# One-hots of the edge sums read from a table, both bias rows written by VectorE, and W1's first half split by GpSimd, in a two-layer graph network kernel

## The chip, the cores and the metric

The kernel runs on one core of a Trainium2 chip. The metric is device time in microseconds (us) of that core, the median of several runs. A core has five engines with queues of their own: TensorE (PE; its weight loads are listed as PEld), VectorE (DVE), ScalarE (ACT), GpSimd (POOL) and SyncE (SP, which here only issues DMAs). They meet through semaphores. "PEq", "DVEq" and "SPq" are the sequencers of the queues.

## The reference, cut to what matters

```python
# x (1250, 512), src and dst (20000,), dst sorted, edge_attr (20000, 64), all float32
h  = relu(layernorm(x))
h0 = (1 + eps) * h + segment_sum(h[src], dst)
h0 = relu(batch_norm(h0 @ W01 + b01))        # 1024 wide
h0 = relu(batch_norm(h0 @ W02 + b02))        # 512 wide, the "second norm"
x  = x + h + h0
h  = relu(layernorm(x))
z1 = concat(h[src], h[dst], edge_attr) @ W1 + b1        # per edge
z2 = mish(z1) @ W2 + b2                                 # per edge
agg = segment_sum(mish(z2), dst)
u  = mish(concat(h, agg) @ W3 + b3)
x  = x + layernorm(h + u @ W4 + b4) * gamma + beta
```

## The kernel before, in words

Everything is float32. Products are made in three terms from operands split into a high part (rounded to the fast matmul type) and a low part (the rest), so each operand needs one cast and one subtraction ahead of its product. Every engine's program is written out by hand; its order is the order of the work, and nothing is scheduled by a planner.

**Stages**, in us of the profiled span: counting edges into a matrix of counts (0 to 92), the first product z0 (to 146), W01 with the first norm (`batch_norm` on VectorE, `move_product` on ScalarE; to 208), W02 with the second norm (to about 266), the layer norm and its transposes, then P = h @ W1[0:512] and Q = h @ W1[512:1024] for all nodes (`pq`, to 332), the first half of W3 with the first edge pairs between (to 365), the edge loop (to about 1020), the last products (to 1094).

**Norm stages.** A product runs feature block by feature block (`o`), each in four pieces (`b`) of 314 nodes. ScalarE moves a piece out of PSUM (line 1274), VectorE takes its statistics (1616). After the fourth piece VectorE aggregates (1621), ScalarE takes the root (1264), VectorE makes scale and shift in four tiny steps that each wait for the one before (1626 to 1629), and ScalarE applies them (1268). The high and low parts of the first norm's result are made on ScalarE (1361) and VectorE (2012) and feed the next product k block by k block. Meanwhile GpSimd splits the edge attributes (`attr_parts`, 724 and 729) in small blocks which SP stores to tables in HBM.

**W1.** ScalarE makes the high part of W1's eight k blocks (`w1_high`, 1378), the first four around the end of the second norm; GpSimd waits for the end of that norm and then makes the low parts (755). P's first product waits for the first four. Until then TensorE runs products that nobody reads (`idle_products`, 878), of which `IDLE_HT` = 4 and `IDLE_PQ` = 7 stand here.

**The edge loop.** A step works on pair `s`, 256 edges in two tiles of 128, 79 pairs in all. Steps are software-pipelined, and in the loops two steps (even and odd `s`) differ. In step `s`:
- TensorE: `z1(s)`, 8 transposes of gathered rows (1099) and 8 attribute products (1106); the second tile of `z2(s-2)` (12 products: 1124, 1125, 1129); the four products of the segment sum of pair `s-4` with its one-hot matrices (1156); the first tile of `z2(s-1)`.
- ScalarE: eight passes over 128x1024 for the two mish functions: 1431, 1435, 1439, then 1455 of pair `s-2`, then 1443, 1459, 1463, 1467.
- VectorE: `full1(s)` in two halves (`h_full`, 2107), high part of the message of `s-3` (2142), high part of h (2117), low part of the message (2146), `message(s-2)` (2132), the two one-hots of `s-2` (`hots1`, 1654), the row b2 into the PSUM bank of the first z2 tile of `s` (`b2_first_tile`, 2136), low part of h (2121). In even steps it then adds the segment sums of four tiles to the nodes (`add_group`, 1665, two instructions), which waits for the segment products of pair `s-3` (made in TensorE's odd step `s+1`), and loads the next group's row numbers into registers (1642).
- The b2 row of the second tile: ScalarE copies it in odd steps (`b2_second_tile`, 1470), for pairs of even number; for pairs of odd number TensorE adds it by a product with ones (1122).
- `z1(s)` waits for `h_full` of pair `s-1`, because both use the same PSUM banks; `full1(s)` waits for ScalarE's last pass on pair `s` (1443); ScalarE's first pass on `s` waits for `z1(s)`.
- GpSimd gathers rows of P and Q from HBM by indirect DMA (766, 774); SP loads the attribute parts (566), four pairs ahead.

## Time and profile before

| | us |
|---|---|
| median of 3 runs | 1096.25 (1095.99 to 1096.29) |
| the profiled execution, its own time | 1095.75 |
| its span, first to last instruction | 1093.9 |
| granted TensorE clock, mean | 0.989 of full speed |
| busy in the span: PE / DVE / ACT / POOL | 1037.2 / 864.4 / 886.2 / 717.4 |

1.85 us of the profiled execution lie around its span. Busy shares are averages over stages with different limits; matmuls overlap each other in the records (a 128x512 product is listed at 0.39 us and the next one starts 0.23 us later), so distances between starts are what counts on TensorE. On VectorE and ScalarE, too, a start can lie a little before the end of the instruction ahead.

### The profile page before, as it was taken

How to read it: one execution, taken by the hardware profiler on the slowest of the kernel's cores; microseconds unless marked ns; L12 is line 12 of the kernel's file. 1: busy time of each engine (PE TensorE's matmuls, PEld its weight loads, DVE VectorE, ACT ScalarE, POOL GpSimd, SP SyncE). 2: the span in 40 equal slices, each digit the busy share in tenths (PEclk: the TensorE clock that was granted, in tenths of full speed). 3: DMA queues.
4: the chain of work that ended last, by engine and by line, in shares of the span. 5: the costliest groups of instructions: out<-in, count | busy, mean ns of one | idle time of the engine just before them, and what ended most of it. 6: DMA issues, size and time to landing. Idle time of an engine off the chain costs nothing.

```text
span 1093.9 us, 18566 instructions
## 1 busy us (share of the span) xinstructions
PE 1037.2 (95%) x5633; PEld 873.0 (80%) x5634; DVE 864.4 (79%) x1500; ACT 886.2 (81%) x1081; POOL 717.4 (66%) x622
## 2 busy tenths in 40 slices
PE   3668999999999999999999999999999999999997
PEld 1226889998889878888888888888888888888796
DVE  7998536635526389999999999999999999999686
ACT  6985735624603699999999999999999999999584
POOL 6874448553255587777777777777777777760227
PEclk9969999999999999999999999999999999999999
DMA  2006962773165387776666676666666666661002
GB/s 106 9 1 151 173 217 93 247 228 116 71 227 119 86 187 161 161 166 136 139 143 146 136 142 145 139 139 138 148 139 138 143 147 134 140 135 39 1 1 95
DMA packets 82914, 141.63 MB, mean 129 GB/s; under 512 B 11115, under 2 KB 39020, under 8 KB 82742
## 3 DMA queue, kind: packets, MB, share of 16 engines
q0 software_dynamic: 38048, 87.58, 39.8%
q1 hardware_dynamic: 44822, 53.52, 15.3%
q8 instruction: 21, 0.34, 0.1%
q14 instruction: 23, 0.19, 0.1%
HBM read 115.42 MB, written 20.39 MB: 124 GB/s over the span
## 4 chain that ended last, share of the span: by engine, by line
PE 85%; DVE 7%; ACT 3%; issue 2%; POOL 1%; DVEq 1%; DMA 1%; ACTq 0%; POOLq 0%
PE banks L1124 12%; PE banks L1125 12%; PE banks L1129 12%; PE banks L1023 9%; PE banks L1156 7%; PE banks L1106 7%; PE banks L1099 6%; PE banks L1066 5%; PE banks L941 4%; PE banks L1087 4%; DVE edge_counts L1799 2%; PE banks L1219 2%; DVE key_onehot L1738 1%; PE banks L996 1%; PE banks L1122 1%
## 5 line engine op out<-in xcount | busy, mean ns | idle before, releaser
L774 POOL DMA_INDIRECT gather_pq<-q_table,dst x157 | 325.2, 2071 | 57.1 <-issue 47.5
L766 POOL DMA_INDIRECT gather_pq<-p_table,src x157 | 174.9, 1114 | 118.6 <-PE banks L1106 67.6
L1124 PE MATMUL banks<-w_lo,h_hi 128*128 128x512 f32 x620 | 242.0, 390 | 0.0
L1125 PE MATMUL banks<-w_hi,h_hi 128*128 128x512 f32 x620 | 241.7, 390 | 0.0
L1129 PE MATMUL banks<-w_hi,h_lo 128*128 128x512 f32 x620 | 166.1, 390 | 0.0
L1129 PEld LDWEIGHTS banks<-w_hi,h_lo 128*128 128x128 f32 x620 | 116.4, 188 | 24.4
L1125 PEld LDWEIGHTS banks<-w_hi,h_hi 128*128 128x128 f32 x620 | 116.4, 188 | 23.7
L1124 PEld LDWEIGHTS banks<-w_lo,h_hi 128*128 128x128 f32 x620 | 116.4, 188 | 23.5 <-issue 0.8
L2107 DVE SCALAR_TENSOR_TENSOR h_full<-mish_work,banks 128x512 f32<-128x512 f32 (+1 forms) x154 | 98.4, 680 | 45.0 <-ACT mish_work L1443 41.2
L2132 DVE SCALAR_TENSOR_TENSOR message<-mish_work,banks 128x1024 f32<-128x1024 f32 x78 | 95.3, 1221 | 8.4 <-ACT mish_work L1467 0.3
L1099 PE MATMUL banks<-ident,gather_pq 128*128 128x128 f32 x628 | 96.5, 275 | 1.5 <-DVE h_full L2107 0.9
L1106 PE MATMUL banks<-edge_attr_parts,we_hi 128*128 128x256 f32 (+1 forms) x316 | 94.6, 321 | 0.0
L2146 DVE TENSOR_TENSOR message_lo<-message,message_hi 128x1024 fp32r<-128x1024 f32 x77 | 93.1, 1209 | 0.0
L2121 DVE TENSOR_TENSOR h_lo<-h_full,h_hi 128x1024 fp32r<-128x1024 f32 (+1 forms) x77 | 93.0, 1208 | 0.0
L1099 PEld LDWEIGHTS banks<-ident,gather_pq 128*128 128x128 f32 x628 | 72.0, 140 | 18.2 <-DVE h_full L2107 11.7
L1467 ACT ACTIVATE mish_work<-mish_work 128x1024 f32<-128x1024 f32 (+1 forms) x79 | 83.5, 1057 | 2.5
L1463 ACT ACTIVATE mish_work<-mish_work 128x1024 f32<-128x1024 f32 (+1 forms) x79 | 83.2, 1054 | 1.3
L1431 ACT ACTIVATE mish_work<-banks 128x1024 f32<-128x1024 f32 (+1 forms) x77 | 78.6, 1021 | 6.7 <-PE banks L1106 5.8
L1435 ACT ACTIVATE mish_work<-mish_work 128x1024 f32<-128x1024 f32 (+1 forms) x77 | 81.4, 1057 | 2.5
L1439 ACT ACTIVATE mish_work<-mish_work 128x1024 f32<-128x1024 f32 (+1 forms) x77 | 81.3, 1056 | 2.4
L1459 ACT ACTIVATE mish_work<-mish_work 128x1024 f32<-128x1024 f32 (+1 forms) x79 | 82.5, 1044 | 0.1
L1106 PE MATMUL banks<-edge_attr_parts,we_lo 128*128 128x256 f32 (+1 forms) x316 | 81.6, 280 | 0.0
(268 smaller groups left out, 2610.6 us busy)
## 6 DMA issues: line engine op xcount, KB each, us to landing
edge_attr<-in_edge_attr_t SPq DMA_DIRECT2D x20, 256.0 KB, 2.9
attr_high<-edge_attr_hi SPq DMA_DIRECT2D x40, 128.0 KB, 2.1
attr_low<-edge_attr_lo SPq DMA_DIRECT2D x40, 128.0 KB, 1.8
edge_attr_parts<-attr_high SPq DMA_DIRECT2D x79, 64.0 KB, 2.8
edge_attr_parts<-attr_low SPq DMA_DIRECT2D x79, 64.0 KB, 3.7
x_nodes<-h_hi POOLq DMA_DIRECT2D x10, 256.0 KB, 15.0
x_nodes<-h_lo POOLq DMA_DIRECT2D x10, 256.0 KB, 7.8
p_table<-p_stage SPq DMA_DIRECT2D x10, 256.0 KB, 2.0
```

Of the source, the lines that this page charges most:

```text
L766: nc.gpsimd.indirect_dma_start(GP[:, 2 * j + k, :], None, p_tab[:, :], bass.IndirectOffsetOnAxis(ap=SRC[:, 2 * s + k:2 * s + k + 1], axis= ...
L774: nc.gpsimd.indirect_dma_start(GP[:, 2 * j + k, :], None, q_tab[:, :], bass.IndirectOffsetOnAxis(ap=DST[:, 2 * s + k:2 * s + k + 1], axis= ...
L1023: mm = pe.matmul(bank, weights[w][:, k, o * P:(o + 1) * P], acts[a](k)[:, nodes], start=(k == 0 and n == 0), stop=(k == kn - 1 and n == 2) ...
L1099: pe.matmul(Z1v[:, c, k * P:(k + 1) * P], GP[:, 2 * slot + k, c * P:(c + 1) * P], IDENT[:, :], is_transpose=True, skip_group_check=True, s ...
L1106: mm = pe.matmul(Z1v[:, c, 0:P * tiles(s)], w[:, c * P:(c + 1) * P], AT_R[:, slot, 0:P * tiles(s)], skip_group_check=True, start=False, st ...
L1124: pe.matmul(at, h_high(s, j)[:, c, e], W2_LO[:, c, :], start=False, stop=False, skip_group_check=True)
L1125: pe.matmul(at, h_high(s, j)[:, c, e], W2_HI[:, c, :], start=False, stop=False, skip_group_check=True)
L1129: mm = pe.matmul(at, h_low(s, j)[:, c, e], W2_HI[:, c, :], start=False, stop=(c == KD - 1), skip_group_check=True)
L2107: nc.vector.scalar_tensor_tensor(h_full_of(s)[:, at[0], at[1]], z1_work(s)[:, at[0], at[1]], -0.5, Z1v[:, at[0], at[1]], ALU.add, ALU.mult ...
L2121: nc.vector.tensor_tensor(h_low(s, j)[:, :, 0:P * tiles(s)], h_full_of(s)[:, :, 0:P * tiles(s)], h_high(s, j)[:, :, 0:P * tiles(s)].bitcas ...
L2132: nc.vector.scalar_tensor_tensor(MSG[:, :, :], EB[:, :, :], -0.5, z2_out(s, j), ALU.add, ALU.mult).then_inc(msg_full, 1)
L2146: nc.vector.tensor_tensor(MSG_LO[:, :, :], MSG[:, :, :], MSG_HI[:, :, :].bitcast(F32), ALU.subtract).then_inc(msg_lo, 1)
```

## The change

- **One-hots from a table.** The one-hots of the edge sums are no longer made in the edge loop. `four_hots` makes those of four tiles with one VectorE instruction (128x512), between the pieces of both norms (22 and 7 times) and behind each of the ten pieces of Q; ScalarE stores each of the 39 blocks (256 KB) to a new table in HBM (`store_hots`); the two staging slots lie in the upper part of the `iota` tile, which GpSimd writes again before the edge loop. In the edge loop SP loads 128 KB per pair, once the sums of two pairs before are made, behind the attribute loads of a pair six further on.
- **b2.** `b2_both_tiles` writes the row into both PSUM banks with one VectorE instruction (128x1024, right behind `message`); ScalarE's copies and the products with ones go, for all pairs from the third.
- **W1.** GpSimd makes high and low parts of the first four k blocks itself: two blocks when the attribute parts are done, the high parts of two more once those are stored, their low parts behind the end of the second norm. ScalarE keeps the high parts of the last four. `IDLE_HT` is 3 and `IDLE_PQ` 4; ScalarE moves the first transposed block ahead of the second root of the layer norm; the load of the b2 row moves behind the stores of P.
- **Scale and shift** in both norms: one of the waits between the four tiny steps goes.

```diff
-IDLE_HT, IDLE_PQ = 4, 7
+IDLE_HT, IDLE_PQ = 3, 4
+HOT_PIECES_1 = [(o, b) for o in range(KH) for b in range(3) if b != 1 or o in (0, 1, 4, 5, 6, 7)]
+HOT_PIECES_2 = [(o, b) for o in range(KD) for b in (0, 2) if (o, b) != (KD - 1, 2)]
 ...
+            def further_hots(q, j):
+                sp.wait_ge(seg_done, q - 1)
+                hots(q, j)
 ...
             for nt in range(NT):
                 sp.wait_ge(q_moved, nt + 1)
                 sp.dma_start(q_tab[nt * P:(nt + 1) * P, :], AGG[:, nt, :]).then_inc(q_stored, 16)
 ...
+            for j in range(2):
+                sp.wait_ge(hots_stored[j], 16 * ((HOT_GROUPS + 1 - j) // 2))
+            for q in range(2):
+                hots(q, q)
 ...
                 for j in range(SLOTS):
                     further_attributes(SLOTS * i + j, j)
+                    further_hots(SLOTS * i + j - HOTS_BEHIND, j % 2)
 ...
-                if after(s, 2) and k == 0:
-                    pe.wait_ge(b2_first, s - 1)
-                elif after(s, 2) and j == 0:
-                    pe.wait_ge(b2_second, s)
+                if after(s, 2):
+                    if k == 0:
+                        pe.wait_ge(b2_seeded, s - 1)
                 else:
                     pe.matmul(at, ONES_R[:, :], B2_R[:, :], start=True, stop=False, skip_group_check=True)
 ...
+                else:
+                    pe.wait_ge(hots_in[j], 16 * (group + 1))
 ...
+            def store_hots():
+
+                g = hots_sent[0]
+                hots_sent[0] += 1
+                act.wait_ge(hots_made, g + 1)
+                nc.scalar.dma_start(hot_tab[2 * g:2 * g + 2, :, :].rearrange("q p e -> p q e"),
+                                    HOTS4[:, g % 2, :, :].rearrange("p (q k) e -> p q (k e)", q=2)).then_inc(hots_stored[g % 2], 16)
 ...
+                        if (o, b - 1) in pieces:
+                            store_hots()
 ...
-                if j == 1 and after(s, 3) and live(s - 1) and tiles(s - 1) == 2:
-                    b2_second_tile(s - 1, 1 - j)
 ...
+            def four_hots():
+
+                g = hots_begun[0]
+                hots_begun[0] += 1
+                if g >= 2:
+                    dve.wait_ge(hots_stored[g % 2], 16 * (g // 2))
+                wide = [P, GROUP, P]
+                nc.vector.tensor_tensor(HOTS4[:, g % 2, :, :], IOTA[:, 0:P].rearrange("p (o k) -> p o k", o=1).broadcast_to(wide),
+                                        REL_G[:, GROUP * g:GROUP * (g + 1)].rearrange("p (t o) -> p t o", o=1).broadcast_to(wide),
+                                        ALU.is_equal).then_inc(hots_made, 1)
 ...
-            def b2_first_tile(s, j):
+            def b2_both_tiles(s, j):
                 dve.wait_ge(msg_full, s - 1)
-                nc.vector.tensor_copy(Z2[:, 2 * j, :], B2_ROW[:, 0, :]).then_inc(b2_first, 1)
+                nc.vector.tensor_copy(Z2[:, 2 * j:2 * j + 2, :], B2_ROW[:, :, :].broadcast_to([P, 2, DIM])).then_inc(b2_seeded, 1)
 ...
-                if live(s - 2):
-                    hots1(s - 2, j)
-                    if live(s):
-                        b2_first_tile(s, j)
+                if live(s - 2) and live(s):
+                    b2_both_tiles(s, j)
```

VectorE in the edge loop, an even step, from `message` to the segment sums; before:

```order
L2132 SCALAR_TENSOR_TENSOR message<-mish_work,banks 128x1024 [waits msg_lo,b_r]
L1654 ISA
L1654 TENSOR_SCALAR onehot<-iota,dst_in_group 128x128
L1654 ISA
L1654 TENSOR_SCALAR onehot<-iota,dst_in_group 128x128
L2136 COPY banks<-b_row 128x512 [waits msg_full]
L2121 TENSOR_TENSOR h_lo<-h_full,h_hi 128x1024 [waits h_hi]
L2152 REGISTER_ALU [waits xagg_done]
L1662 ISA [waits seg_done,agg_done]
L1665 REGISTER_ALU
L1665 SCALAR_TENSOR_TENSOR agg_nodes<-banks,from_low,agg_nodes 128x512
```

The same place after the change:

```order
L2234 TENSOR_TENSOR message_lo<-message,message_hi 128x1024 [waits msg_hi]
L2220 SCALAR_TENSOR_TENSOR message<-mish_work,banks 128x1024 [waits msg_lo,b_r]
L2224 COPY banks<-b_row 128x1024 [waits msg_full]
L2213 TENSOR_TENSOR h_lo<-h_full,h_hi 128x1024 [waits h_hi]
L2240 REGISTER_ALU [waits xagg_done]
L1752 ISA [waits seg_done,agg_done]
L1755 REGISTER_ALU
L1755 SCALAR_TENSOR_TENSOR agg_nodes<-banks,from_low,agg_nodes 128x512
```

Both one-hots are gone, the copy is twice as wide, and it now stands directly behind the instruction whose end (`msg_full`) it waits for.

GpSimd from the last attribute parts over the end of the second norm (`bn_ready`) to the gathers of P; before:

```order
L729 TENSOR_TENSOR edge_attr_lo<-edge_attr,edge_attr_hi 128x256 [waits attr_low_stored1,attr_hi]
L755 TENSOR_TENSOR w_lo<-weights_a,w_hi 128x512 [waits w1_hi_made,bn_ready]
L755 TENSOR_TENSOR w_lo<-weights_a,w_hi 128x512 [waits w1_hi_made] x7
L766 DMA gather_pq<-p_table,src 128x512 [waits p_stored,idx_in]
```

The same place after the change:

```order
L795 CAST w_hi_first_half<-weights_a 128x512 [waits w1_in,attr_lo]
L795 CAST w_hi_first_half<-weights_a 128x512
L799 TENSOR_TENSOR w_lo<-weights_a,w_hi_first_half 128x512 [waits w1_first_hi_made] x2
L795 CAST w_hi_first_half<-weights_a 128x512 [waits attr_low_stored0,attr_low_stored1,attr_high_stored1,attr_high_stored0]
L795 CAST w_hi_first_half<-weights_a 128x512
L799 TENSOR_TENSOR w_lo<-weights_a,w_hi_first_half 128x512 [waits w1_first_hi_made,bn_ready]
L799 TENSOR_TENSOR w_lo<-weights_a,w_hi_first_half 128x512 [waits w1_first_hi_made]
L817 TENSOR_TENSOR w_lo<-weights_a,w_hi 128x512 [waits w1_hi_made] x4
```

Six instructions now stand ahead of the end of the norm, and two instead of four of the low parts that P waits for stand behind it.

## Rows read from the trace of the kernel before

**Rows 1.** Busy time by engine: us, busy (count) per engine, clock, DMA, GB/s.

```profile
400.00:1010.00 610.00, 609.41 (x3239) 515.05 (x3238) 559.46 (x803) 600.15 (x621) 452.41 (x279) 1.00 0.67 140
```

**Rows 2.** TensorE in order of time, edge loop: start, us, instruction, count.

```profile
703.15 0.66 PE L1099 MATMUL banks<-ident,gather_pq 128*128 128x128 f32 x4
704.91 0.28 PE L1106 MATMUL banks<-edge_attr_parts,we_lo 128*128 128x256 f32 x1
...
711.45 0.60 PE L1099 MATMUL banks<-ident,gather_pq 128*128 128x128 f32 x4
...
713.26 0.40 PE L1122 MATMUL banks<-b_parts,ones 128*128 128x512 f32 x1
713.50 0.39 PE L1124 MATMUL banks<-w_lo,h_hi 128*128 128x512 f32 x1
...
716.92 0.39 PE L1156 MATMUL banks<-message_lo,onehot 128*128 128x512 f32 x1
```

**Rows 3.** ScalarE in the same stretch.

```profile
702.64 0.59 ACT L1470 COPY banks<-b_row 128x512 f32<-128x512 f32 x1
705.22 1.03 ACT L1431 ACTIVATE mish_work<-banks 128x1024 f32<-128x1024 f32 x1
```

**Rows 4.** VectorE in the same stretch.

```profile
702.41 1.28 DVE L2107 SCALAR_TENSOR_TENSOR h_full<-mish_work,banks 128x512 f32<-128x512 f32 x2
...
710.33 1.28 DVE L2107 SCALAR_TENSOR_TENSOR h_full<-mish_work,banks 128x512 f32<-128x512 f32 x2 [0.85 <-ACT mish_work L1443]
...
712.75 1.20 DVE L2146 TENSOR_TENSOR message_lo<-message,message_hi 128x1024 fp32r<-128x1024 f32 x1
714.05 1.22 DVE L2132 SCALAR_TENSOR_TENSOR message<-mish_work,banks 128x1024 f32<-128x1024 f32 x1
715.19 0.47 DVE L1654 TENSOR_SCALAR onehot<-iota,dst_in_group 128x128 fp32r<-128x128 f32 x2
715.59 0.68 DVE L2136 COPY banks<-b_row 128x512 f32<-128x512 f32 x1
716.18 1.21 DVE L2121 TENSOR_TENSOR h_lo<-h_full,h_hi 128x1024 fp32r<-128x1024 f32 x1
717.66 0.75 DVE L1665 SCALAR_TENSOR_TENSOR agg_nodes<-banks,from_low,agg_nodes 128x512 f32 x1 [0.26 <-issue]
```

**Rows 5.** Single lines over 400 to 1000: durations in ns (min/median/max), first and last start.

```profile
L1665 DVE SCALAR_TENSOR_TENSOR agg_nodes<-banks,from_low,agg_nodes x35: 750/751/752, 416.3 to 985.5; 128x512 f32 x35
```

**Rows 6.** VectorE, the first such sum, an earlier stretch of the edge loop.

```profile
397.56 1.22 DVE L2121 TENSOR_TENSOR h_lo<-h_full,h_hi 128x1024 fp32r<-128x1024 f32 x1
...
398.73 0.75 DVE L1665 SCALAR_TENSOR_TENSOR agg_nodes<-banks,from_low,agg_nodes 128x512 f32 x1
```

**Rows 7.** DVE's sequencer over 400 to 1000, the register load behind the sums.

```profile
L1642 DVEq TENSOR_LOAD <-tile_range x36: 743/748/1451, 399.3 to 986.1; - x36
```

**Rows 8.** All engines around the end of the second norm.

```profile
251.96 1.44 POOL L729 TENSOR_TENSOR edge_attr_lo<-edge_attr,edge_attr_hi 128x256 fp32r<-128x256 f32 x2
...
266.31 4.98 POOL L755 TENSOR_TENSOR w_lo<-weights_a,w_hi 128x512 fp32r<-128x512 f32 x4 [12.92 <-DVE bn_shift L1629]
...
269.24 0.83 DVE L1607 SCALAR_TENSOR_TENSOR ln_bias<-ln_mean_var,rstd 128x2 f32<-128x2 f32 x1
```

**Rows 9.** The same, a little later.

```profile
272.58 0.16 DVE L1607 SCALAR_TENSOR_TENSOR ln_bias<-ln_mean_var,rstd 128x4 f32<-128x4 f32 x1
272.76 0.69 DVE L1635 SCALAR_TENSOR_TENSOR h_t_lo<-banks,h_t_hi 128x512 fp32r<-128x512 f32 x1
...
273.80 0.39 PE L1066 MATMUL banks<-w_hi,h_t_lo 128*128 128x512 f32 x1
```

**Rows 10.** ScalarE and VectorE at the end of the first norm.

```profile
199.12 1.43 ACT L1268 ACTIVATE hidden_t<-hidden_t,bn_shift,bn_scale 128x1256 f32<-128x1256 f32 x1
200.99 0.49 DVE L1616 BATCH_NORM_STATS2 bn_stats<-hidden_t 128x6 f32<-128x314 f32 x1 [1.25 <-ACT hidden_t L1274]
...
202.70 0.48 DVE L1616 BATCH_NORM_STATS2 bn_stats<-hidden_t 128x6 f32<-128x308 f32 x1 [1.23 <-ACT hidden_t L1274]
```

**Rows 11.** DMA issues of the page: KB each, median us to landing.

```profile
edge_attr<-in_edge_attr_t SPq DMA_DIRECT2D x20, 256.0 KB, 2.9
```

**Rows 12.** TensorE at the first edge pair.

```profile
343.15 0.66 PE L1099 MATMUL banks<-ident,gather_pq 128*128 128x128 f32 x4 [0.53 <-DMA gather_pq<-q_table,dst]
```

More of the change, by code:

```diff
@@ L394, in gnn_kernel @@
         gat1 = [sem(f"gathered1_{j}") for j in range(SLOTS)]
-        hot_ready, seg_done, agg_done = sem("hot_ready"), sem("seg_done"), sem("agg_done")
+        seg_done, agg_done = sem("seg_done"), sem("agg_done")
+        hots_made, hots_stored, hots_in = sem("hots_made"), [sem(f"hots_stored{j}") for j in range(2)], [sem(f"hots_in{j}") for j in range(2)]
         last_hots = sem("last_hots")
@@ L751, in _, with w1_first_hi, w1_first_lo @@
             attr_parts(ATTR_FIRST, ALL_STEPS)
+            def w1_first_hi(k):
+                nc.gpsimd.tensor_copy(W1P_HI[:, k, :], WA[:, k, :]).then_inc(w1p_hi, 1)
+            def w1_first_lo(k):
+                pool.wait_ge(w1p_hi, k + 1)
+                nc.gpsimd.tensor_tensor(W1_LO[:, k, :], WA[:, k, :], W1P_HI[:, k, :].bitcast(F32), ALU.subtract).then_inc(w1_lo, 1)
+            pool.wait_ge(attr_lo, 2 * ALL_STEPS)
+            pool.wait_ge(w1_in, 16)
+            w1_first_hi(0)
+            w1_first_hi(1)
+            w1_first_lo(0)
+            w1_first_lo(1)
+            for stored in attr_stored:
+                for j in range(2):
+                    pool.wait_ge(stored[j], 16 * ALL_STEPS)
+            w1_first_hi(2)
+            w1_first_hi(3)
             pool.wait_ge(bn_ready, KH + KD)
-            for k in range(2 * KD):
-                pool.wait_ge(w1_hi, k + 1)
+            w1_first_lo(2)
+            w1_first_lo(3)
+            for k in range(KD, 2 * KD):
+                pool.wait_ge(w1_hi, k - KD + 1)
                 nc.gpsimd.tensor_tensor(W1_LO[:, k, :], WA[:, k, :], W1_HI[:, k, :].bitcast(F32), ALU.subtract).then_inc(w1_lo, 1)
@@ L790, in _ @@
                 gather_q(s)
+            for j in range(2):
+                pool.wait_ge(hots_stored[j], 16 * ((HOT_GROUPS + 1 - j) // 2))
+            nc.gpsimd.iota(IOTA[:, P:NP], [[1, NP - P]], base=P, channel_multiplier=0,
+                           allow_small_or_imprecise_dtypes=True).then_inc(pool_const, 1)
             for s in range(SLOTS, EDGE_PAIRS):
@@ L1064, in pq @@
                 for k in range(KD):
-                    for a, w in ((HT_LO, W1_HI), (HT_HI, W1_LO), (HT_HI, W1_HI)):
-                        mm = pe.matmul(Z2[:, 2 * part + nt % 2, :], a[:, k, nt * P:(nt + 1) * P], w[:, KD * part + k, :],
-                                       start=(k == 0 and a is HT_LO), stop=(k == KD - 1 and a is HT_HI and w is W1_HI))
+                    high = W1_HI[:, KD + k, :] if part else W1P_HI[:, k, :]
+                    for n, (a, w) in enumerate(((HT_LO, high), (HT_HI, W1_LO[:, KD * part + k, :]), (HT_HI, high))):
+                        mm = pe.matmul(Z2[:, 2 * part + nt % 2, :], a[:, k, nt * P:(nt + 1) * P], w,
+                                       start=(k == 0 and n == 0), stop=(k == KD - 1 and n == 2))
                 mm.then_inc(mm_done, 1)
@@ L1135, in _, with segment1 @@
             FINAL_ROWS = [FINAL_MSG.rearrange("p c e -> p (c e)")]
-            def segment1(s, j, last):
+            def segment1(s, j, last, group):
                 final = isinstance(s, int) and s == FINAL
@@ L1175, in edge_step @@
                 if live(s - 4):
-                    segment1(s - 4, j, j == 1 or isinstance(s, int) and s - 4 == EDGE_PAIRS - 1)
+                    segment1(s - 4, j, j == 1 or isinstance(s, int) and s - 4 == EDGE_PAIRS - 1, group)
                 if live(s - 1):
@@ L1425, in _ @@
             nc.scalar.preload_act_table_set("natural_log_exp_and_others")
+            for _ in range(HOT_TABLE):
+                store_hots()
+            assert hots_sent[0] == HOT_GROUPS
             def exp1(s):
@@ L2122, in lo1 @@
                                         h_high(s, j)[:, :, 0:P * tiles(s)].bitcast(F32), ALU.subtract).then_inc(h_lo, 1)
-            def hots1(s, j):
-                make_hots([ONEHOT[:, j, k, :] for k in range(2)], REL_G, 2 * s).then_inc(hot_ready, 1)
             def message(s, j):
```

79 lines of the change are left out of this document (52 added, 27 removed).

## The prediction

> **What bounds the kernel now.** Read first the busy time of the edge loop [rows 1]. In 610 us TensorE is busy for 609.4, ScalarE for 600.2, VectorE for 559.5: three engines that are nearly full, so the loop is bound by a round trip through several of them, and busy shares don't say which. The loop is also most of the kernel: the sums of line 1665 stand once in two pairs, and 34 of their intervals fill 985.5 - 416.3 us [rows 5], so two pairs take 16.74 us, and about 37 such periods follow each other.
>
> Read then who waits, in order of time, through one period. VectorE waits visibly only in even steps: h_full at 710.33 for ScalarE, 0.85 us [rows 4]. The other h_full, at 702.41, starts late behind the sums, and TensorE's transposes of the next pair start at 703.15 [rows 2], 0.74 later: half an h_full. That is TensorE's only stall in the period, and small: the record shows those four transposes 0.66 long and the unstalled ones at 711.45 0.60 long, and with the last 0.02 us of waiting it is about 0.08 in all. So TensorE alone needs 16.66 of 16.74.
>
> Two round trips can be read off, both through that h_full.
> - **Path B, by TensorE.** Transposes 703.15, last segment product 716.92 + 0.39 = 717.31 [rows 2], sums 717.66 (0.35 later), the next h_full 702.41 + 16.74 = 719.15 (1.49 later), transposes 0.74 later: 14.16 + 0.35 + 1.49 + 0.74 = 16.74. This path is tight.
> - **Path A, by VectorE and ScalarE.** h_full 710.33 to h_lo 716.18 is 5.85; from h_lo the sums could start 1.17 later, as they did at 398.73 behind the h_lo of 397.56 [rows 6], where they even overlap its end by 0.05; then 1.49 and 0.74 as above; transposes 703.15 to ScalarE's first pass 705.22 [rows 3] is 2.07; that to h_full 710.33 is 5.11. The sum is 16.43, so this path has 0.31 us to spare. The profile calls the 0.26 ahead of the sums "issue", which looks like VectorE's own time; I read it as the wait for TensorE.
>
> **The change part by part, edge loop.** *TensorE* loses the b2 product of every second pair: 713.50 - 713.26 = 0.24 per period [rows 2]. It lies in path B: 16.50. TensorE alone: 16.66 - 0.24 = 16.42. *ScalarE* loses its copy of 0.59 (702.64, rows 3). It is in no tight path: ScalarE's pass of 705.22 starts when the transposes and attribute products are done (704.91 + 0.28 = 705.19, rows 2), with or without the copy. Worth nothing. *VectorE*, per step: the two one-hots go, 715.59 - 715.19 = -0.40. The copy gets twice as wide: h_full moves 512 columns per instruction in 0.64 and message 1024 in 1.22, so I take 1.22 instead of 0.68: +0.54. And the copy now stands right behind the message whose end it waits for. Without such a wait the next start lies 1.14 behind the message's (715.19 - 714.05); message itself waits for the end of message_lo ahead of it and starts 1.30 behind that one's start (714.05 - 712.75, for 1.20 us of work) [rows 4]. So +0.18. Sum per step -0.40 + 0.54 + 0.18 = +0.32. In odd steps 0.85 us of waiting hides it. In even steps it lies in path A: 16.43 + 0.32 = 16.75.
>
> One link of path A gets shorter with it. The 1.49 from sums to h_full is not VectorE's work (two sums of 0.75 that overlap by 0.08 make 1.33 or so) but its sequencer's: behind the sums it loads registers for 0.75 us [rows 7], and that starts when TensorE's segment products are done. These come 0.24 earlier, the sums 0 to 0.1 later, so the load falls under the sums; the link is then between 1.32 and 1.49. Path A is between 16.58 and 16.75. I take 16.58, since in rows 6 the queue ran ahead of the engine. Against 16.74 that is 0.16 x 37 = **-5.9 us**; the ends are 0 and, if path B or TensorE alone is the bound, -0.24 x 37 = -8.9 to -0.32 x 37 = -11.8.
>
> The Trainium skill, "VectorE: DVE Perf Modes", section "The DRAIN you can't avoid", says that a semaphore between two VectorE instructions costs nothing extra and that only their number counts. By that the +0.18 would be zero, path A 16.40 and path B the bound, -8.9 us. Rows 4 speak against it: 1.30 with a wait, 1.14 without.
>
> The loads of the one-hots (128 KB per pair on SP, behind a wait for the sums of two pairs before) I cost at nothing: a load is issued after the segment products of one step and needed two steps later, two times 8.37 us, against 2.9 for 256 KB to land [rows 11]. The DMA engines are at 0.67 in the loop [rows 1]; 128 KB in 8.4 us is 16 GB/s on 140. If the cover were gone, TensorE would stall at the segment products, by what is missing, 37 times.
>
> **Norms.** *End of the second norm.* Of the low parts of W1, four run from 266.31 for 4.98 us [rows 8], and the tiny ln_bias at 269.24 takes 0.83 beside them, against 0.16 at 272.58 when GpSimd is idle [rows 9]. Two low parts remain there, done by about 268.9, so -0.67. The shorter chain and ScalarE's casts that go give 0.2 more. P starts at 273.80 behind h_t_lo (272.76 + 0.69) and seven idle products; with four of them h_t_lo decides, which gives 0.1. Together **-0.9**. Cover: GpSimd has 266.3 - 253.4 = 12.9 us free there [rows 8] and the six instructions put there need at most 6 x 1.25 = 7.5, at the price of the low parts. Ends: -1.4, and +2 if the attribute parts finish 7 us later because the stores of the one-hots (29 x 256 KB in 110 us) compete with theirs.
>
> *End of the first norm.* The last three blocks of one-hots stand between the last statistics. The store of the first one is issued behind ScalarE's apply, at 199.12 + 1.43 = 200.55 [rows 10], and lands 2.9 later [rows 11], 203.5. The third block uses the same slot, so VectorE, free at 201.5, waits until 203.5 and takes 0.69 more (as h_t_lo, also 128x512, rows 9), to 204.2; the last statistics (202.70) stand behind it, 1.4 late, and ScalarE, which has to issue the third store before its next high part (202.57), is late by as much. TensorE can start the second product with the blocks that are ready; how long they last no row here says, so I take half of the 1.4, **+0.7**, ends -0.3 (shorter chain, store lands in 2) and +2. In the middle of both norms the same waits occur, but TensorE writes into four banks and gets far ahead: nothing.
>
> *Q and the first pair.* TensorE waits 0.53 for the gather of the first pair [rows 12]; the last one-hot store and the first loads now run beside the last store of Q and that gather. All of it is on the path: **+0.5**, ends 0 and +2. The ten one-hot blocks of that stage stand behind what TensorE waits for: nothing.
>
> **The rivals.**
> 1. *TensorE's side is the bound* (the wait costs nothing, or the links overlap more): -8.9 - 0.9 + 0.7 + 0.5 = -8.6, to -11.5 with TensorE alone: 1087.6 to 1084.7. The page's rule on semaphores, above, leads to the first of the two.
> 2. *The sequencer sets the pace*: the link stays 1.49, path A is 16.75, the loop gains nothing: 0 + 0.3 = about 1096.6. For it: the two paths are then equal to the hundredth. Against it: rows 6.
> 3. *Slower: the idle ahead of the sums is VectorE's own.* Then path A has been tight at 16.74 all along, and the +0.32 adds to it: +11.8 + 0.3, or 1108.4. It decides from the point where h_lo's end, and not the last segment product, releases the sums. For it: the word "issue" in rows 4. Against it: rows 6, where no idle time is left.
> 4. *The stores hold up the norms*: attribute parts late, low parts of W1 late, first norm's end +2, first pair +2: the gain is eaten, 1095 to 1099.
>
> **How the numbers follow.** The profiled execution took 1095.75, the median 1096.25; the sum -5.9 - 0.9 + 0.7 + 0.5 = -5.6 is taken from the median: **1090.6**. Chances: forecast (1087.7 to 1094.0) 0.50, rival 1 0.15, rival 2 0.17, rival 3 0.08, rival 4 0.10. The range for 8 in 10 runs from TensorE's bound to rival 4, 1084.5 to 1098.5. A measurement tells about 0.2% (2.2 us) from no change. Faster: forecast and rival 1, 0.65. Within 0.2%: rival 2 and half of rival 4, 0.22. Slower: rival 3 and the other half, 0.13.
>
> **What the profile after would show.** Period of the sums 16.58 (16.50 or less: rival 1; 16.74: rival 2; 17.06: rival 3). Copy of 1024 columns 1.22 long, starting 1.3 behind message. Sums starting at h_lo's end less 0.05, with no idle time. TensorE stalled once per period by 0.15 to 0.2. No ScalarE copy of b2. P's first product about 0.9 earlier behind the second norm; the first norm's end up to 1 later. Wrong would make it above all a VectorE copy of another length, or segment products that wait for a table load.

## The result and the profile after

The changed kernel takes 1143.62 us (1140.15 to 1145.55), the kernel before, in the same session, 1096.27 (1095.99 to 1096.48): a ratio of 1.042, 95% interval 1.040 to 1.044. The forecast was 1090.6, the range 1084.5 to 1098.5, with 0.13 for slower. The measured time lies 53 us above the forecast, and on the other side of the kernel before.

The profiled execution took 1145.55, its span is 1143.7, 49.8 more than before. First the distance between matching instructions of both traces, to see in which stage the time went:

| stage | before | after | more |
|---|---|---|---|
| up to the first product of the first norm | 146.4 | 149.3 | 2.9 |
| that norm's products | 55.4 | 63.6 | 8.2 |
| to the first product with W1 | 72.0 | 76.4 | 4.4 |
| the products P and Q | 58.0 | 66.8 | 8.7 |
| from there to the first sum of the edge loop | 66.9 | 66.6 | -0.3 |
| first to last sum of the loop | 626.6 | 652.5 | 25.9 |

The first row is no effect of the change: the program up to there is the same, and in the kernels below that point lies anywhere from 146.7 to 149.7 (the latter in scan_before, which has nothing of the change). What is left has two parts: 26 us in the edge loop, 21 us ahead of it.

**The edge loop.** VectorE in the even step, from `message` (2220) to the next h_full (2199), in the trace of after; it answers to [rows 4].

```profile
750.90 1.22 DVE L2220 SCALAR_TENSOR_TENSOR message<-mish_work,banks 128x1024 f32<-128x1024 f32 x1
752.15 1.23 DVE L2224 COPY banks<-b_row 128x1024 f32<-128x1024 f32 x1
753.29 1.24 DVE L2213 TENSOR_TENSOR h_lo<-h_full,h_hi 128x1024 fp32r<-128x1024 f32 x1
754.45 0.74 DVE L1755 SCALAR_TENSOR_TENSOR agg_nodes<-banks,from_low,agg_nodes 128x512 f32 x1
755.11 0.74 DVE L1755 SCALAR_TENSOR_TENSOR agg_nodes<-banks,below_low,agg_nodes 128x512 f32 x1
756.88 1.29 DVE L2199 SCALAR_TENSOR_TENSOR h_full<-mish_work,banks 128x512 f32<-128x512 f32 x2 [1.03 <-issue]
```

Down to the sums this is the prediction: the copy is 1.23 long and starts 1.25 behind `message`, the sums start 0.08 before h_lo's end. But h_full stands 2.43 behind them, and not 1.32 (over the steady loop 1.76 to 2.53, median 2.36). What lies between is the register load on DVE's sequencer, with its durations in ns (min/median/max) from 400 to 1000; the row answers to [rows 7].

```profile
L1732 DVEq TENSOR_LOAD <-tile_range x34: 762/1600/1759, 403.4 to 983.4; - x34
```

It took 748 ns before and takes 1600 now, in the same place and for the same three words. TensorE stands still meanwhile; the waits of 400 to 1000 (us in total, times, longest) and its first transposes behind the h_full above:

```profile
PEld banks L1166 <- DVE h_full L2199: 37.7, 33, 1.4
ACT mish_work L1511 <- PE banks L1173: 34.7, 53, 1.2
DVE h_full L2199 <- issue: 29.1, 32, 1.1
...
757.62 0.66 PE L1166 MATMUL banks<-ident,gather_pq 128*128 128x128 f32 x4 [0.83 <-DVE h_full L2199]
```

Path A with what is measured: 16.43 + 0.27 for VectorE's step (from the end of message_lo to h_lo it is 2.50, in before 2.23) + (2.36 - 1.49) for the link = 17.57; the loads of the steady loop stand 17.53 apart. One row of before had already shown the price. Behind the very sum of [rows 6] the next h_full is this one of before, 2.21 later, and its load is the 1451 of [rows 7]:

```profile
400.94 1.28 DVE L2107 SCALAR_TENSOR_TENSOR h_full<-mish_work,banks 128x512 f32<-128x512 f32 x2 [0.80 <-issue]
```

**The first norm.** SP, VectorE, ScalarE and TensorE from 155 to 167, after:

```profile
155.64 1.94 SPq L556 DMA_DIRECT2D weights_b<-in_w  x4
...
165.03 0.69 DVE L1692 TENSOR_TENSOR onehots_of_group<-iota,dst_in_group 128x512 f32<-128x512 f32 x1 [6.50 <-DMA onehot_table<-onehots_of_group]
...
166.18 0.52 ACT L1352 ACTIVATE hidden_t<-banks,cols 128x314 f32<-128x314 f32 x1 [7.31 <-DVE onehots_of_group L1692]
...
166.97 0.60 PE L1089 MATMUL banks<-z_t_lo,w_hi 128*128 x1 [3.51 <-ACT hidden_t L1352]
```

The third block waits 6.5 us for the store of the first, issued at 156.93 between the third and the fourth load of 512 KB of weights (155.64 to 157.10). ScalarE waits for the block before it moves the next piece, and TensorE, four banks ahead, still stands for 3.5 us. Behind that its granted clock is 0.50 (1.2 of 2.4 GHz) from 167 to 170, against 1.00 in before, and the products are 0.26 apart instead of 0.145. Five short stands between 178 and 209, 2.4 us in all, make up the rest of the 8.2.

**P and Q.** VectorE and GpSimd ahead of the fifth piece of Q, and from the waits of 290 to 358 that of TensorE, after:

```profile
335.79 6.41 DVE L1692 TENSOR_TENSOR onehots_of_group<-iota,dst_in_group 128x512 f32<-128x512 f32 x1 [1.72 <-DMA onehot_table<-onehots_of_group]
342.12 0.68 DVE L2185 TENSOR_TENSOR agg_nodes<-banks,rows 128x512 f32<-128x512 f32 x1
...
334.48 2.29 POOL L846 CAST w_lo<-weights_a 128x512 fp32r<-128x512 f32 x4
336.73 4.92 POOL L849 TENSOR_TENSOR w_hi<-weights_a,w_lo 128x512 fp32r<-128x512 f32 x4
...
PE banks L1133 <- DVE agg_nodes L2185: 5.7, 1, 5.7
```

One block takes 6.41 us in place of 0.69. It starts while GpSimd works through eight instructions without a pause and ends 0.55 behind the last of them. Behind TensorE's wait of 5.7 us its granted clock is 0.50 from 343.0 to 347.7, and eleven products stand 0.43 apart instead of 0.23: that is 2.2 us more of the 8.7.

### The profile page after: what moved, and what is told of

The parts are those of the page before. It is cut to its first block and busy times, and to the rows that moved or that the text cites. A ratio compares the mean times of both kernels' runs of the same rounds, so it can differ in the third digit from the quotient of the medians.

```text
span 1143.7 us, 18499 instructions
## 1 busy us (share of the span) xinstructions
PE 1051.8 (92%) x5591; PEld 868.1 (76%) x5592; DVE 910.0 (80%) x1385; ACT 872.6 (76%) x1039; POOL 655.8 (57%) x627
## 3 DMA queue, kind: packets, MB, share of 16 engines
q1 hardware_dynamic: 55910, 63.62, 18.6%
## 5 line engine op out<-in xcount | busy, mean ns | idle before, releaser
L836 POOL DMA_INDIRECT gather_pq<-q_table,dst x157 | 262.1, 1670 | 65.4 <-issue 47.6
L828 POOL DMA_INDIRECT gather_pq<-p_table,src x157 | 171.9, 1095 | 209.3 <-PE banks L1173 158.3
L1190 PE MATMUL banks<-w_lo,h_hi 128*128 128x512 f32 x620 | 245.5, 396 | 0.3 <-DVE banks L2224 0.3
L2224 DVE COPY banks<-b_row 128x1024 f32<-128x1024 f32 x77 | 94.5, 1228 | 2.6
```

Source lines behind the costliest of these rows:

```text
L828: nc.gpsimd.indirect_dma_start(GP[:, 2 * j + k, :], None, p_tab[:, :], bass.IndirectOffsetOnAxis(ap=SRC[:, 2 * s + k:2 * s + k + 1], axis= ...
L836: nc.gpsimd.indirect_dma_start(GP[:, 2 * j + k, :], None, q_tab[:, :], bass.IndirectOffsetOnAxis(ap=DST[:, 2 * s + k:2 * s + k + 1], axis= ...
L1190: pe.matmul(at, h_high(s, j)[:, c, e], W2_LO[:, c, :], start=False, stop=False, skip_group_check=True)
L2224: nc.vector.tensor_copy(Z2[:, 2 * j:2 * j + 2, :], B2_ROW[:, :, :].broadcast_to([P, 2, DIM])).then_inc(b2_seeded, 1)
```

## The experiments

All times are medians; the ratio goes by the runs of before of the same session.

### What makes the register load long

The first theory, *queue*: the load is long whenever VectorE's sequencer has run ahead, that is when h_lo and not TensorE releases the sums. Its rival, *traffic*: the 128 KB of one-hots land beside it.

**b2_only.** The kernel before, one-hots in the loop, both rows by VectorE.

```diff
-                nc.vector.tensor_copy(Z2[:, 2 * j, :], B2_ROW[:, 0, :]).then_inc(b2_first, 1)
+                nc.vector.tensor_copy(Z2[:, 2 * j:2 * j + 2, :], B2_ROW[:, :, :].broadcast_to([P, 2, DIM])).then_inc(b2_seeded, 1)
...
-                elif after(s, 2) and j == 0:
-                    pe.wait_ge(b2_second, s)
...
-                    b2_second_tile(s - 1, 1 - j)
```

> The kernel before with one edit: both bias rows written by VectorE (128x1024), ScalarE's copy and the product with ones gone; one-hots still made in the loop, no table. Per step VectorE gets 0.54 us more, so path A is 16.97 us with the old link from sums to h_full, and the sums are released by h_lo and no longer by TensorE. Theory 'queue' (the register load behind the sums takes about 1.6 us instead of 0.75 whenever the sums did not have to wait for TensorE): load about 1.6, h_full about 2.4 behind the sums, two pairs in about 17.9 us, 37 x 1.15 more, about 1139. Theory 'traffic' (the load is long because the 128 KB of one-hots land beside it): load stays 0.75, two pairs in 16.97, about 1105.

1124.8 us, ratio 1.024 (1.022 to 1.026), two pairs in 17.61. The load's row from 400 to 1000:

```profile
L1635 DVEq TENSOR_LOAD <-tile_range x35: 761/1455/1526, 400.4 to 997.8; - x35
```

There is no table here and the load is long: *traffic* falls. The two bias rows alone cost 28 us, where about 42 were expected.

**table_only.** The changed kernel with the bias rows as before (the diff above, backwards).

> The changed kernel with the bias rows written as before (VectorE 512 columns, ScalarE's copy, product with ones); the table, its stores and loads and the split of W1 stay. VectorE's step gets about 0.24 us shorter than before. Theory 'queue': the sums wait for TensorE again, the load is 0.75, two pairs take 16.74 as before, and what is left is the loss ahead of the edge loop: about 1118 to 1122. Theory 'traffic': the load is still about 1.6, two pairs in about 17.5, about 1145.

1117.3, ratio 1.017 (1.014 to 1.020), two pairs in 16.79. The load is 0.75 with all one-hot loads in place:

```profile
L1740 DVEq TENSOR_LOAD <-tile_range x36: 745/750/1151, 404.6 to 996.2; - x36
```

**load_odd.** The changed kernel, the load moved.

```diff
-                    load_range(0, i - 1)
+                    for n in range(R_USED):
+                        dve.reg_mov(range_regs[0][n], range_regs[1][n])
+                if live(s - 1) and j == 1:
+                    load_range(1, i)
```

> The changed kernel with the register load moved from behind the sums to the end of the odd step, where VectorE waits for ScalarE anyway, into a second set of three registers; three register moves stand behind the sums instead. Theory 'queue': h_full stands about 1.4 behind the sums again, two pairs in 16.6 to 16.75, about 1108 to 1112. Theory 'traffic': the load in its new place is 0.75, since no one-hots land there, and the time is the same. Third theory (the load is a symptom, the loop is long because VectorE's step is): two pairs stay at 17.6, 1143.

1112.9, ratio 1.013 (1.010 to 1.016): 31 us less than the changed kernel, two pairs in 16.62. The place of the load in its even step, which has no idle time left:

```profile
754.46 1.22 DVE L2213 TENSOR_TENSOR h_lo<-h_full,h_hi 128x1024 fp32r<-128x1024 f32 x1
755.60 0.74 DVE L1755 SCALAR_TENSOR_TENSOR agg_nodes<-banks,from_low,agg_nodes 128x512 f32 x1
756.26 0.74 DVE L1755 SCALAR_TENSOR_TENSOR agg_nodes<-banks,below_low,agg_nodes 128x512 f32 x1
756.92 1.27 DVE L2199 SCALAR_TENSOR_TENSOR h_full<-mish_work,banks 128x512 f32<-128x512 f32 x2
```

The link is 1.32, the lower end of the prediction, and the period 0.04 from its 16.58. So the loss of the loop is the load's, and VectorE's longer step is paid for. But one of the 36 loads is 1282 long, at 412.8, where there is no sum ahead at all. *Queue* cannot say why. Laid beside each other, the traces had another thing in common: GpSimd's gathers of Q. Here in after, beside the load that runs from 755.0 to 756.7, and in before, beside the one from 718.2 to 718.95:

```profile
753.26 1.57 POOL L836 DMA_INDIRECT gather_pq<-q_table,dst  x1 [0.30 <-issue]
755.14 1.56 POOL L836 DMA_INDIRECT gather_pq<-q_table,dst  x1 [0.31 <-issue]
...
716.40 2.44 POOL L774 DMA_INDIRECT gather_pq<-q_table,dst  x1 [0.30 <-issue]
```

In after, the load begins 0.18 behind the end of one gather and 0.13 ahead of the next. In before it begins inside a gather, which lasts 2.44. That made a third theory, *gather*.

**gather_later.** The changed kernel; only GpSimd is touched.

```diff
                 gather_p(s)
+                for _ in range(3 if s % 2 else 0):
+                    if padded:
+                        pool.wait_ge(pad_sem, padded)
+                    nc.gpsimd.memset(PAD[:, :], 0.0).then_inc(pad_sem, 1)
+                    padded += 1
                 gather_q(s - 1)
```

> The changed kernel with one edit on GpSimd: in every second pair three small memsets (128x184) stand between the gathers of P and those of Q, so that the gather of Q that started 0.13 us behind VectorE's register load starts about 0.8 later. New theory 'gather' (from the four traces so far: the load behind the sums takes 1.4 to 1.7 us where an indirect gather starts within 0.3 us behind its start, and 0.75 elsewhere, whatever released the sums): load 0.75, h_full 1.5 behind the sums, two pairs in 16.6 to 16.8, about 1112. Theory 'queue' (it is long because the sums did not wait for TensorE): load still 1.6, two pairs 17.5, about 1143.

1117.0, ratio 1.018 (1.016 to 1.020), 27 us less than the changed kernel, two pairs in 16.71. VectorE's program is that of the changed kernel, the sums still wait for nobody, and the load is short. *Queue* falls.

```profile
L1739 DVEq TENSOR_LOAD <-tile_range x36: 745/750/1431, 403.8 to 992.6; - x36
```

**scan_before.** The kernel before, with (s // 2) % 8 such memsets in place of three.

> The kernel before with 0 to 7 small memsets (128x184) on GpSimd between the gathers of P and of Q of every second pair, the number rising by one from one such pair to the next and falling back to 0 after 7: the gathers of Q slide over VectorE's register load in steps of about 0.25 us, while the sums ahead of that load still wait for TensorE. Theory 'gather': the load is 0.75 where no gather starts in the first 0.5 us of it, and 1.0 to 1.7 where one does. Theory 'queue': 0.75 at every position. The time: a few us above before in the first case, the same in the second.

1099.8 in one run. The load is 0.75 at every position of the steady loop, also in the four cases where a gather starts 0.15 to 0.22 behind it. So the start of a gather does it no harm, and my reading of *gather* was wrong in this half.

**scan_after.** The changed kernel, memsets ahead of the first gather of Q and between the two.

```diff
+            AHEAD = (0, 1, 2, 3, 0, 1, 2, 3, 0, 1, 2, 3)
+            BETWEEN = (0, 0, 0, 0, 1, 1, 1, 1, 3, 3, 3, 3)
                 for k in range(tiles(s)):
+                    if s >= SLOTS and s % 2 == 0:
+                        padding(BETWEEN[(s // 2) % 12] if k else AHEAD[(s // 2) % 12])
```

> The changed kernel with GpSimd's two gathers of Q moved in every second pair by small memsets: 0 to 3 ahead of the first, and 0, 1 or 3 between the two, twelve combinations in turn. So far every long load of the steady loop began in the pause between the two gathers of Q, less than 0.25 us behind the end of the first and less than 0.3 ahead of the start of the second. Theory 'pause' (both are needed): long loads at 0 ahead, 0 between, and short ones as soon as the start lies inside a gather or the pause is filled. Theory 'end of the first gather': long at every combination with 0 ahead, also where memsets stand between. Theory 'queue': long everywhere.

1121.7 in one run. From 436 on there are 34 loads. Eight are long (1.21 to 1.68 us), all eight at 0 ahead, whether 0, 1 or 3 memsets stand between; at each, the first gather had ended 0.07 to 0.17 us before. The other 26 are 0.74 to 0.78, and at each of them that gather was still running when the load began, and ended 0.47 to 1.02 us behind its start. One case of each, first the gathers, then the load (duration and start in its row), 0 ahead and 3 between:

```profile
485.51 1.58 POOL L850 DMA_INDIRECT gather_pq<-q_table,dst  x1 [0.30 <-issue]
486.50 1.47 POOL L841 MEMSET pad<- 128x184 f32 x3
488.13 1.57 POOL L850 DMA_INDIRECT gather_pq<-q_table,dst  x1 [0.16 <-issue]
...
L1746 DVEq TENSOR_LOAD <-tile_range x1: 1674/1674/1674, 487.2 to 487.2; - x1
```

and 1 ahead, with VectorE's h_lo:

```profile
570.74 1.22 DVE L2227 TENSOR_TENSOR h_lo<-h_full,h_hi 128x1024 fp32r<-128x1024 f32 x1
...
570.84 2.57 POOL L850 DMA_INDIRECT gather_pq<-q_table,dst  x1 [0.16 <-issue]
573.72 1.66 POOL L850 DMA_INDIRECT gather_pq<-q_table,dst  x1 [0.30 <-issue]
...
L1746 DVEq TENSOR_LOAD <-tile_range x1: 747/747/747, 572.5 to 572.5; - x1
```

The second gather 0.93 us behind the load's start (first case) leaves it long, so *pause* falls and *end of the first gather* stands. A gather that starts 1.6 to 1.7 before the load can go either way: it ends in time and the load is long (622.5: 1.21), or it takes 2.57 and the load is short (572.5).

**Which way it goes.** The load does not lengthen the gather: in before the first gather of Q lasts 2.44 in the odd steps too, 7 us away from any load. What does is `h_lo`, VectorE's subtraction with both inputs in SBUF:

```profile
620.84 1.60 POOL L850 DMA_INDIRECT gather_pq<-q_table,dst  x1 [0.30 <-issue]
...
620.88 1.22 DVE L2227 TENSOR_TENSOR h_lo<-h_full,h_hi 128x1024 fp32r<-128x1024 f32 x1
```

This gather starts 0.04 ahead of h_lo and takes 1.60. The one at 570.84 starts 0.10 behind h_lo's start and ends 1.45 behind its end. So it is in all 16 traces (430 to 985 us): the 636 gathers of Q that start inside h_lo end 1.41 to 1.47 behind its end, and the 294 that start up to 0.10 ahead of it take 1.57 to 1.60.

This also says why the change moved the gather. GpSimd's gather of P that starts inside `message_lo`, a subtraction of the same kind, ends 0.84 to 0.90 behind its end (973 cases), and the first gather of Q of an even step follows at a fixed distance: it starts 2.45 or 2.46 us behind message_lo's end in before, after and table_only alike (medians). h_lo starts 2.23 behind it in before, 2.50 in after and 1.96 in table_only. With the wide copy h_lo therefore no longer starts 0.22 ahead of the gather but 0.04 behind it; the gather is not held, and its end falls 0.18 ahead of the load's start instead of 0.64 behind it. In table_only h_lo is 0.50 ahead of it, and the load is short; in b2_only it is 0.05 behind it, and the load is long.

### The stages ahead of the loop

**w1_only.** The changed kernel without table and with the old bias rows.

```diff
+HOT_PIECES_1 = []
+HOT_PIECES_2 = []
+HOT_TABLE = 0
...
-                    b2_both_tiles(s, j)
+                    hots1(s - 2, j)
+                    if live(s):
+                        b2_first_tile(s, j)
```

> The changed kernel without table, stores and loads (one-hots made in the loop by VectorE) and with the bias rows written as before: what is left is the split of W1 by GpSimd, fewer idle products and the shorter scale-and-shift chain. If the stages ahead of the loop lose by the stores of the table alone: TensorE's first product with W1 at about 273 us, 1095 to 1096. If they lose by these edits: that product late by several us, above 1100.

1094.8, ratio 0.9986 (0.9976 to 0.9997). From the first product of the first norm to the first one with W1 it is 124.3 us, against 127.4 before; the first norm itself takes 55.4 in both. The split of W1 pays, 1.9 us in the median, and the whole loss ahead of the loop is the table's.

**hots_no_stores.** The blocks are made, and ScalarE waits for them, but nothing is stored or loaded.

```diff
-                nc.scalar.dma_start(hot_tab[2 * g:2 * g + 2, :, :].rearrange("q p e -> p q e"),
-                                    HOTS4[:, g % 2, :, :].rearrange("p (q k) e -> p q (k e)", q=2)).then_inc(hots_stored[g % 2], 16)
...
-                    dve.wait_ge(hots_stored[g % 2], 16 * (g // 2))
+                    dve.wait_ge(hots_made, g - 1)
```

> The changed kernel with the 39 blocks of one-hots still made between the pieces (VectorE's work and ScalarE's waits for it stay), but not stored and not loaded; the edge loop makes its own one-hots and writes the bias rows as before. Theory 'store wait' (ahead of the loop the time goes to blocks that wait until the store of the same slot has landed): TensorE's first product with W1 at 273 to 276 instead of 289. Theory 'work' (VectorE's 0.7 us per block and the longer chain to ScalarE is what holds TensorE): 282 or later. For the stage of Q: the block that took 6.41 us at 335.8 began while GpSimd ran eight instructions without a pause; if GpSimd holds it up, a block of 3 us or more is there without any store too, and TensorE waits for it; if the stores did it, all blocks are 0.7. Total 1098 to 1104 by the first of each.

1103.8 in one run. The first norm's products take 55.4 us again, and the first product with W1 starts at 274.0: *store wait* is right. The blocks' own work is free in the first norm; from its first product to the first one with W1 it is 126.6 us, 2.3 more than in w1_only and 13.3 less than in after. P and Q take 63.8, still 5.8 more, and here is the long block without any store:

```profile
319.69 7.81 DVE L1676 TENSOR_TENSOR onehots_of_group<-iota,dst_in_group 128x512 f32<-128x512 f32 x1
...
319.72 2.29 POOL L827 CAST w_lo<-weights_a 128x512 fp32r<-128x512 f32 x4
321.97 4.97 POOL L830 TENSOR_TENSOR w_hi<-weights_a,w_lo 128x512 fp32r<-128x512 f32 x4
```

**w3a_paced.** load_odd, with pauses between GpSimd's eight instructions.

```diff
             for k in range(KD):
+                pool.wait_ge(hots_made, HOT_GROUPS - 7 + k // 2)
                 nc.gpsimd.tensor_copy(W3A_HI[:, k, :], WA[:, k, :]).then_inc(w3a_hi, 1)
             for k in range(KD):
+                pool.wait_ge(hots_made, HOT_GROUPS - 5 + k)
```

> The kernel load_odd (1112.9) with one edit on GpSimd: its eight instructions on W3 in the stage of Q no longer run without a pause, each waits for a further block of one-hots to be made. Theory 'held off' (a VectorE instruction with two SBUF inputs that meets GpSimd's instructions waits until a pause between them): no block above 2 us in that stage, TensorE's wait of about 5.7 us there goes, 1106 to 1109. If the long block comes from VectorE's own instruction at that place: still 6 to 7 us, 1113.

1107.6, ratio 1.012 (1.009 to 1.015). That is 5.3 less than load_odd in the medians, but the two ranges overlap (1104.5 to 1112.8 and 1107.3 to 1115.1); the stage itself tells more. P and Q take 61.0 in place of 66.6, and no block is above 1.54:

```profile
L1694 DVE TENSOR_TENSOR onehots_of_group<-iota,dst_in_group x39: 666/692/1535, 154.3 to 346.2; 128x512 f32<-128x512 f32 x39
```

So GpSimd's unbroken run held VectorE. The Trainium skill, "SBUF — State Buffer", section "Who interferes with whom", says that a VectorE instruction with two inputs in SBUF and a GpSimd instruction that reads SBUF exclude each other for a whole instruction, and that whoever is first has the port. The trace agrees that they exclude each other and adds the price here: the block stood until all eight had gone, 7.8 us, and not one of them. Which was first the trace doesn't settle: in hots_no_stores the block's record starts 0.03 ahead of GpSimd's first. P and Q are still 3.0 longer than in before, with TensorE waiting for single blocks (1.5 us at most).

### What the loop gains without the load

**before_load_odd.** The kernel before with load_odd's diff alone.

> The kernel before with the register load alone moved to the odd step (three register moves behind the sums). By path B as the prediction read it, the link from sums to h_full falls from 1.49 to about 1.32, and then TensorE alone is the bound at 16.66 in place of 16.74: 37 x 0.08 = 3 us less, about 1093.5. If path B was not tight: no change.

1093.0, ratio 0.9978 (0.9963 to 0.9993), two pairs in 16.63. As read: path B was tight by the load. That TensorE alone comes next was my reading; 16.63 lies 0.03 under the 16.66 that I had put down for it.

**w1_load_odd.** w1_only and load_odd's diff.

> The two parts that paid, together: W1 split by GpSimd with the shorter chain, and the register load in the odd step; one-hots, bias rows as before. 1.9 + 3.4 less than before: 1090.5 to 1092.

1090.0, ratio 0.9953 (0.9934 to 0.9972). The two gains add up. TensorE is busy for all of the 610 us.

**odd_both.** In addition VectorE writes both rows in odd steps, behind the one-hots.

```diff
+                if j == 1:
+                    nc.vector.tensor_copy(Z2[:, 2:4, :], B2_ROW[:, :, :].broadcast_to([P, 2, DIM])).then_inc(b2_first, 1)
...
-                else:
+                elif not after(s, 2):
```

> Built from the readings so far: no table, W1 split by GpSimd, register load in the odd step, and VectorE writes both bias rows in the odd step only, where it waits 0.85 us for ScalarE and two one-hots part the copy from the message; in even steps ScalarE's copy of the second row stays. TensorE's product with ones goes: TensorE alone 16.42, path B 16.74 - 0.24 - 0.17 = 16.33, path A 16.43 - 0.17 = 16.26 plus nothing in even steps. Two pairs in 16.42 to 16.55, 37 x 0.2 to 0.3 less, and 1.9 from the split of W1: 1083 to 1088. If the odd step's longer copy is on a path after all: 16.7 or more, 1094 or above.

1095.3, ratio 0.999 (0.998 to 1.000), two pairs in 16.76: a miss. TensorE's first z2 product waited for the wide copy, 18.6 us in 37 times.

**odd_first.** The wide copy ahead of the one-hots.

```diff
+                    if live(s) and j == 1:
+                        b2_first_tile(s, j)
                     hots1(s - 2, j)
-                    if live(s):
+                    if live(s) and j == 0:
```

> The combination odd_both with one swap: in the odd step the 128x1024 bias copy stands ahead of the two one-hots instead of behind them. In odd_both TensorE waited 0.5 us per two pairs for that copy (ended 757.64, product at 757.78); now it ends about 0.3 earlier. Two pairs in 16.45 to 16.6, 1086 to 1091. If something else holds that product, 16.76 again, 1095.

1090.5, ratio 0.9949 (0.9929 to 0.9968), two pairs in 16.63. TensorE still waits 12.8 us for it in all.

**odd_split.** The first row where it was, the second of odd pairs behind h_lo.

```diff
                     lo1(s, j)
+                if live(s - 2) and live(s) and j == 1:
+                    nc.vector.tensor_copy(Z2[:, 3, :], B2_ROW[:, 0, :]).then_inc(b2_odd, 2)
```

> w1_load_odd (1090.0), and VectorE writes the second bias row of odd pairs by itself, 128x512 behind h_lo of the odd step, where it waits 1.0 us for ScalarE; the first row stays where it was, so TensorE's first tile no longer waits for a wide copy as in odd_first (12.8 us of waiting in 37 periods). TensorE's product with ones goes, 0.24 per two pairs, from a loop in which TensorE never waits: 16.64 to between 16.40 and 16.50, 37 x 0.14 to 0.24 less, 1081 to 1085. If ScalarE alone is the bound by then (busy for 599 of 610 us): 16.45 to 16.55, 1083 to 1087. If the copy delays h_full: 16.6 or more, 1090.

1086.75 us (1086.3 to 1089.1), ratio 0.9919 (0.9896 to 0.9941), two pairs in 16.55. It is the fastest kernel here, 9.7 us under the one before and 57 under the changed one. Its row of 400 to 1010, to be read beside [rows 1]:

```profile
400.00:1010.00 610.00, 609.79 (x3231) 510.61 (x3230) 586.89 (x850) 599.66 (x626) 463.45 (x281) 1.00 0.65 140
```

The 0.24 of TensorE bought 0.09. What bounds the loop now is open: from 430 to 1000 neither TensorE nor ScalarE has a gap above 0.04 us, but that was so in w1_load_odd too, with its 16.64.

## Why the prediction was wrong

- **The failed step** is the link of path A: "the load falls under the sums; the link is then between 1.32 and 1.49", with the reason that in rows 6 the queue ran ahead. The link is 2.36 in the median. I looked at the start of that sum and not at the next h_full, 2.21 behind it, and I passed over the 1451 in rows 7, which belongs to it. The range had no bound for a load longer than 0.75. With 0.87 more per two pairs, path A gives 17.57 with the measured 0.27 for VectorE's step; measured are 17.53.
- **What the load depends on** was in no step: the phase of GpSimd's gathers. I counted what VectorE and TensorE do and took GpSimd, which no path waits for, as absent. The phase is set by VectorE's own message_lo and h_lo, so the +0.32 that I put on VectorE's step did more than lengthen path A: it moved h_lo past the gather's start.
- **Right in the loop:** the copy (1.22 forecast, 1.23), its wait (1.30 forecast; 1.25 behind `message`, against 1.14 without a wait in [rows 4], so a wait costs 0.11 here), the sums at h_lo's end, no ScalarE copy, and nothing lost to the loads of the one-hots. load_odd shows what the sum would have been without the failed link: 16.62 for 16.58. The Trainium skill, "VectorE: DVE Perf Modes", section "The DRAIN you can't avoid", says that a semaphore between two VectorE instructions costs nothing extra; the measured 0.11 differs from that, and the measurement decides.
- **Rival 3** (slower, +11.8) had the sign and less than half of the loop's 25.9, by another cause: path A had 0.31 to spare, as load_odd shows, and the "issue" ahead of the sums was the wait for TensorE. **Rival 4** had the right kind of cause, stores that hold up the norms, but its +2 for the first norm's end is 8.2 for the norm.
- **"In the middle of both norms the same waits occur, but TensorE writes into four banks and gets far ahead: nothing"** failed. The landing of 2.9 us was the median of 20 loads; among the loads of W02's 2 MB the first store took 8.1 us, and a wait of 7.3 us is longer than four banks last. The trace of before had shown it: behind a load of 2 MB issued at 208.92, five transfers of 128 and 256 KB issued from 209.70 to 214.61 took 8.2 to 11.6 us to land. Both norms together, +12.6 for a forecast of -0.2.
- **"The ten one-hot blocks of that stage stand behind what TensorE waits for: nothing"** failed too, +8.7: each block stands ahead of VectorE's next piece, and one was held for 6.4 us by GpSimd's work on W3.
- **W1** was right in sign and short in size: -0.9 forecast, -1.9 in w1_only's median (-3.1 from the first norm's first product to the first one with W1).
- The loss is 25.9 in the loop and 21.0 from the first norm to the loop, and 2.9 lie ahead of everything that was changed.

## What to carry to other kernels

A shorter stall or a longer step on one engine shifts everything behind it in time, also against engines that no path waits for: before an edit on a tight path, look at what every other engine does at the moment of each short sequencer instruction on it, and get that instruction off the path if it can stand where the engine waits anyway. When a rare row of the trace shows the state that a change will make the rule, read on from it to the end of the path, and use the maximum of its group, not the median. Here 0.27 us more on VectorE decided which of two engines starts first, and that cost 26 us. Staging through two slots is only as fast as the slowest store, which is the one behind the largest load of the stage.

## What the runs showed of the hardware

- A load of three registers from SBUF on VectorE's queue takes 0.74 to 0.80 us, with engine and DMA busy or not (0.75 in before_load_odd, where VectorE was at work and the DMA engines were busy for 0.75 of the time during the loads), and longer behind one of GpSimd's gathers of Q. In all 16 traces, from 360 to 1100 us, the 90 loads that start 0.04 to 1.06 us behind the end of such a gather take 1.04 to 1.76, and the 550 others, 2.04 or more behind one, never more than 0.80. The 90 include the long loads at the start of the loop (1451 in [rows 7], and eleven like it in ten other kernels). The end of a gather of P does no harm: 219 loads start 0.65 to 0.93 behind one and are short. What the load and the gather share isn't shown, nor why P's gathers differ.
- An indirect gather that starts while a 128x1024 `tensor_tensor` of VectorE with both inputs in SBUF runs ends 1.41 to 1.47 us behind that instruction's end for Q (636 cases) and 0.84 to 0.90 for P (973); one of Q that starts up to 0.10 ahead of it takes 1.57 to 1.60 (294). This gives the 2.44 in before, the 2.16 in table_only and the 1.57 with the wide copy.
- A 128x512 `tensor_tensor` of VectorE with both inputs in SBUF took 6.3 to 7.8 us beside eight GpSimd instructions without a pause (six kernels), 0.69 alone, and at most 1.54 with pauses between GpSimd's instructions (w3a_paced). The additions of the pieces of Q, with one input in PSUM, stood beside the same eight in before and took 0.69.
